# A gated state-space layer on one core: five fill banks and one bank for y, the fill three tiles ahead, 32-row pieces, and jobs in a new order

## The chip, the cores and the metric

One core of a Trainium2 chip runs the whole program. The time is the device time of that core in microseconds (us). A kernel's time is the median of several runs; the profile shows one further execution.

## The reference, cut to what matters

```python
xr, gate = jnp.split(x @ W_in.T, 2, axis=-1)            # x: (2, 2048, 512), 1024 channels each
xc = silu(causal_conv4(xr + t_emb, W_conv) + b_conv)    # depthwise, 4 taps
xn = (xc - mean) / sqrt(var + 1e-5) * ln_g + ln_b
Bm, Cm, dt = jnp.split(xn @ W_xproj.T, 3, axis=-1)      # 16 states each
Ad = 1.0 - tanh(A_log) * 0.01 * tanh(dt @ W_dt.T + b_dt)
Bd = Bm * minimum(norm(xn), 1.0)
# for each token t:
h = clip(h * ad[:, :, None] + bd[:, :, None] * xt[:, None, :], -10.0, 10.0)
y = einsum('bd,bdh->bh', ct, h) + D * xn
out = x + (y * silu(gate)) @ W_out.T
```

## The kernel before

The two sequences of 2048 tokens are cut into chunks of 128 tokens, taken in turn from the two sequences: 32 steps. `steps` runs the bodies for k = -2 to 32. In the body of step k the core does the scan of chunk k, and in the gaps the preparation of the chunks k+1 (the norm, the state at the chunk's head, the stacks) and k+2 (projection, convolution, statistics) and the output of chunk k-1. 30 steps (k = 0 to 29) hold all of this.

A step has 32 tiles, 8 blocks of 128 channels times 4 groups of 4 states. A tile goes through six stages, each counted by a semaphore:

- `fill` (L539, TensorE, PE): four matmuls from the row stack `xs` and the weights `ts` into one bank of `ps_fill`. They give the lower bound of the clipped scan.
- `copy_low` (L769, ScalarE, ACT) copies the bank to `low`.
- `widen` (L548, PE) adds the span to the same bank, which makes the upper bound.
- `scan` (L975, VectorE, DVE) runs the clipped scan over `low` and the bank.
- `weigh` (L1073, GpSimd, POOL) multiplies by C.
- `flip` (L575, PE) transposes four 128x128 blocks and adds them into `ps_y`. Before the tiles 0 and 16 it starts a half of y with `base` (L555), and before the tiles 12 and 16 it adds D times xn with `skip` (L561).

In iteration s PE runs widen(s+1), fill(s+2), the jobs of point 2s, flip(s-4) and the jobs of point 2s+1; ACT runs copy_low(s+2) and `side` of both points; DVE runs scan(s+1) and its `side`; POOL runs weigh(s) and one side instruction in some iterations. Every queue is in order. `ps_fill` has 4 banks and `fill` of a tile waits until the tile 4 before it was scanned. `ps_y` has 2 banks, one for each half (512 channels) of y. `gated` (L963, DVE) multiplies a half of y by the gate; `base` of a half waits until `gated` has read that half of the chunk before.

`JOBS` lists the other matmuls as (first point, parts, name, half, chunk offset, halves, bank of `ps_job`); a job's parts lie at successive points, and the share of its work in a part is worked out by integer division. A job waits until the job before it in its bank was taken. `TAKE` is the point at which ACT or DVE reads the result, `TAP_AT` the points at which ACT makes the eight channel blocks of the convolution's taps. The chunk k+1 side work on DVE is: z (L869, L873), zm (L900), the decay scan pf (L904), its reciprocal (L923), h0 (L919), bc (L927), the four nb instructions (L937 to L944), the clip of h1 (L931, point 28) and the carries (L955). `xt` is the transposed xc, from which z is made; ACT takes its second half at point 62 and the first gate job uses the same bank.

SyncE (SP) issues all transfers in one order. The stack `xs` of the next chunk is loaded in body k after `xh_done`: for each 32-token block two copies of `xh` rows 1 to 31 (L340, L341) and one of the 32 rows of `xl` (L345). Rows 0 and 32 of the stack hold ones, loaded once in `later_loads`. ACT's `carry` (L745) and DVE's (L955) write into the tiles `xh` and `xl`, so they wait for `xstack_in`. Further down SP issues the pieces of `ts` (L379, 31 and 32 rows), the carry rows (L383) and h16 (L388).

Of the kernel before, what the change touches and what calls it, by code (L numbers as in the profile page):

```python
# [26 lines left out]
P = 128  # L27
# [3 lines left out]
SUB = 32  # L31
NSUB = P // SUB
# [7 lines left out]
RING = 4  # L40
AHEAD = 2
LAG = 4
HOLD = 4
TAPRING = 4
# [27 lines left out]
xstack_in0 xstack_in1 stack_in0 stack_in1 bound_out bound_in0 bound_in1  # L72
# [13 lines left out]
def build(nc, A, out, scratch, r_dram, c_dram):  # L86
    F, H = mybir.dt.float32, mybir.dt.float16
    ALU, ACT = mybir.AluOpType, mybir.ActivationFunctionType
    with ExitStack() as S:
# [95 lines left out]
        ps_y = S.enter_context(nc.psum_tensor("ps_y", [P, 2, BANK], F))  # L185
        ps_job = S.enter_context(nc.psum_tensor("ps_job", [P, 2, BANK], F))

        def since(eng, name, value):

            if isinstance(value, int) and value <= 0:  # L190
# [7 lines left out]
        JOBS = [(1, 3, "z", 0, 1, 1, 1), (1, 4, "gate", 0, 0, 2, 0), (5, 1, "hend", 0, -1, 2, 1),  # L198
                (6, 4, "gate", 1, 0, 2, 0), (7, 1, "hend", 1, -1, 2, 1), (10, 1, "yT", 1, -1, 2, 1),
                (15, 1, "zT", 0, 1, 1, 1), (17, 4, "xr", 0, 2, 2, 0), (20, 1, "h0", 0, 1, 2, 1),  # L200
                (22, 4, "xr", 1, 2, 2, 0), (23, 1, "h0", 1, 1, 2, 1), (26, 1, "nb", 0, 1, 1, 1),
                (28, 12, "conv", 0, 2, 2, 0), (30, 1, "carry", 0, 1, 2, 1), (34, 1, "carry", 1, 1, 2, 1),
                (38, 14, "out", 0, -1, 1, 1), (44, 10, "conv", 1, 2, 2, 0), (54, 1, "yT", 0, 0, 2, 1),
                (57, 1, "xt", 0, 2, 2, 0), (60, 1, "xt", 1, 2, 2, 0)]
        LAST = {(name, i): first + parts - 1 for first, parts, name, i, *_ in JOBS}
        TAKE = {("z", 0): 4, ("gate", 0): 5, ("hend", 0): 5, ("hend", 1): 7, ("yT", 1): 10, ("gate", 1): 11,
                ("zT", 0): 15, ("h0", 0): 20, ("h0", 1): 23, ("xr", 0): 20, ("nb", 0): 26,
                ("xr", 1): 25, ("carry", 0): 30, ("carry", 1): 34, ("conv", 0): 42, ("out", 0): 52,
                ("conv", 1): 54, ("yT", 0): 54, ("xt", 0): 58, ("xt", 1): 62}
        TAP_AT = [22, 28, 32, 36, 38, 40, 44, 46]  # L210

        Z_AT = 12
        GATED_AT = (42, 8)
# [42 lines left out]
        N_FIXED = 16 * 9  # L256
# [17 lines left out]
        def _(sp):  # L274
# [14 lines left out]
            def later_loads():  # L289
# [4 lines left out]
                for p in range(2):  # L294
                    carry = A["carry"].rearrange("r (j c) -> r j c", j=NSUB)
                    loads.append((ts[96:128, p], carry))
                    for r in (0, 32):
                        loads.append((xs[r:r + 1, p], A["ones16"].rearrange("o (j d) -> o j d", j=NSUB)))
# [8 lines left out]
            def body(k, p):  # L307
# [21 lines left out]
                if exists(k, 1):  # L329
# [8 lines left out]
                    for jj in range(NSUB):  # L338
                        a = SUB * jj
                        sp.dma_start(xs[1:SUB, pn, jj], xh[a + 1:a + SUB]).then_inc(xstack, 16)  # L340
                        sp.dma_start(xs[SUB + 1:2 * SUB, pn, jj], xh[a + 1:a + SUB]).then_inc(xstack, 16)  # L341
# [4 lines left out]
                if exists(k, 1):  # L346
# [9 lines left out]
                    for h in range(2):  # L356
# [7 lines left out]
                                 ).then_inc(sem["c_in"], 16)  # L364
                    sp.wait_ge(sem["bound_out"], 48 * (j + 1))
# [35 lines left out]
        def _(pe):  # L401
# [123 lines left out]
            def fill(k, p, s):  # L525
# [3 lines left out]
                if s == 0:  # L529
                    if isinstance(k, int) and k == 0:  # L530
                        pe.wait_ge(sem["fixed_in"], N_FIXED)
                    pe.wait_ge(sem[f"xstack_in{p}"], N_XSTACK * pair(k, p, 0))
# [4 lines left out]
                o = ps_fill[:, s % RING].rearrange("d (n t) -> d n t", n=QN)  # L537
# [6 lines left out]
            def widen(k, p, s):  # L544
# [3 lines left out]
                mm(ps_fill[:, s % RING], pick[:], spans[:, p, q * BANK:(q + 1) * BANK], start=False, stop=True,  # L548
                   skip_group_check=True).then_inc(sem["bounded"], 1)

            def base(k, p, i):

                half = slice(i * BANK, (i + 1) * BANK)
                since(pe, "y_gated", 2 * (k - 1) + i + 1)
                mm(ps_y[:, i], mT[:, p], xn[:, p, half], start=True, stop=False)  # L555

            def skip(k, p, i):
# [3 lines left out]
                last = mm(ps_y[:, i], ident, xd[:, i * BANK:(i + 1) * BANK], start=False, stop=False)  # L561
# [3 lines left out]
            def flip(k, p, s):  # L565
# [8 lines left out]
                for e in range(QN):  # L574
                    last = mm(ps_y[:, u // 4, cut], prod[:, s % HOLD, e, :], ident, start=False,  # L575
# [30 lines left out]
        def _(act):  # L606
# [21 lines left out]
            def side(k, p, point):  # L628
# [47 lines left out]
                if point == 12 and exists(k, 2):  # L676
# [24 lines left out]
                if point == 24 and exists(k, 1):  # L701
# [418 lines left out]
```

## Time and profile before

| | us |
|---|---|
| median of 3 runs (2226.87 to 2229.91) | 2229.75 |
| the profiled execution | 2229.9 |
| its span, first to last instruction | 2228.1 |

| engine | busy us | share of the span |
|---|---|---|
| PE matmul | 2016.9 | 91% |
| POOL | 1818.6 | 82% |
| DVE | 1762.9 | 79% |
| ACT | 1434.6 | 64% |

Busy times of PE count pipelined matmuls until their modelled ends, so the start-to-start distances in a timeline tell its work better than the busy column. "Idle before, releaser" names what an engine's instruction waited for. The granted clock was 1.0 of full (2.4 GHz) but for the first part of the run.

### The profile page before, as it was taken

The numbers are of one execution on the slowest core, as the hardware profiler recorded it, in microseconds if no ns is written. First come the engines' busy times: TensorE is split into PE (matmuls) and PEld (weight loads), VectorE is DVE, ScalarE is ACT, GpSimd is POOL, SyncE is SP. The second block draws the span as 40 slices with busy tenths as digits, with TensorE's granted clock in tenths as the row PEclk, the third lists the DMA queues.
The fourth block names the chain that finished last, engine by engine and source line by source line (L and its number), as shares of the span: only waits on it lengthen the run. The fifth ranks groups of instructions, "written<-read, shape, count | busy, mean of one in ns | idle before, by whom it ended". The sixth has DMA issues, their size and how long they took to land.

```text
span 2228.1 us, 47105 instructions
## 1 busy us (share of the span) xinstructions
PE 2016.9 (91%) x16976; PEld 1458.5 (65%) x16976; DVE 1762.9 (79%) x2080; ACT 1434.6 (64%) x3462; POOL 1818.6 (82%) x1444
## 2 busy tenths in 40 slices
PE   5599999999999999999999999999999999999888
PEld 4366666666666666666666666666666666666654
DVE  2388888788888788888788888788888878888886
ACT  4576666676666676666666666666666667666642
POOL 1288888888888888888888898888888888888876
PEclk8599999999999999999999999999999999999999
DMA  4111111121111121111111111111111112111110
GB/s 164 51 56 42 53 40 51 57 61 46 49 41 51 56 60 46 50 41 51 56 60 47 51 45 46 55 60 56 44 53 40 53 59 61 40 55 39 46 53 15
DMA packets 77777, 117.05 MB, mean 53 GB/s; under 512 B 17941, under 2 KB 46997, under 8 KB 72933
## 3 DMA queue, kind: packets, MB, share of 16 engines
q1 hardware_dynamic: 77544, 114.04, 16.5%
q8 instruction: 135, 2.21, 0.4%
q14 instruction: 98, 0.79, 0.1%
HBM read 59.47 MB, written 9.18 MB: 31 GB/s over the span
## 4 chain that ended last, share of the span: by engine, by line
PE 35%; SPq 23%; ACT 13%; DMA 12%; issue 8%; DVE 6%; POOL 2%; DVEq 0%; POOLq 0%; ACTq 0%
DMA xs<-xl 11%; SPq L340 9%; SPq L341 9%; PE ps_job L490 7%; PE ps_y L575 6%; SPq L345 5%; PE ps_job L449 5%; PE ps_fill L548 4%; ACT low L769 4%; ACT tap L728 4%; PE ps_fill L539 3%; DVE ks L975 3%; PE ps_job L456 2%; PE ps_job L462 2%; POOL prod L1073 2%
## 5 line engine op out<-in xcount | busy, mean ns | idle before, releaser
L1073 POOL TENSOR_TENSOR prod<-ks,crep 128x512 f32<-128x512 f32 x1024 | 1305.1, 1288 | 292.3 <-PE ps_y L575 265.6
L975 DVE TENSOR_TENSOR_SCAN ks<-low,ps_fill 128x512 f32<-128x512 f32 x1024 | 1227.7, 1210 | 284.1 <-PE ps_fill L548 274.6
L769 ACT COPY low<-ps_fill 128x512 f32<-128x512 f32 x1024 | 594.0, 580 | 594.4 <-PE ps_fill L539 588.3
L575 PE MATMUL ps_y<-c_sb,prod 128*128 128x128 f32 x4096 | 621.3, 274 | 0.7 <-POOL prod L1073 0.6
L575 PEld LDWEIGHTS ps_y<-c_sb,prod 128*128 128x128 f32 x4096 | 465.9, 141 | 113.1 <-issue 50.9
L548 PE MATMUL ps_fill<-spans,pick 128*128 128x512 f16 x1024 | 393.2, 384 | 121.1 <-ACT low L769 117.1
L539 PEld LDWEIGHTS ps_fill<-ts,xs 128*128 128x128 f16 x4096 | 314.4, 98 | 150.2 <-issue 4.9
L539 PE MATMUL ps_fill<-ts,xs 128*128 128x128 f16 x4096 | 397.0, 219 | 2.9 <-DMA xs<-h 2.9
L548 PEld LDWEIGHTS ps_fill<-spans,pick 128*128 128x128 f16 x1024 | 99.3, 97 | 236.4 <-ACT low L769 193.7
L728 ACT ACTIVATE tap<-xr,cols_sb 128x128 f32<-128x128 f32 x768 | 251.7, 392 | 0.1
L444 PE MATMUL ps_job<-x,w_in 128*128 128x128 f16 x3072 | 215.2, 221 | 15.3 <-POOL x L1043 7.8
L490 PE MATMUL ps_job<-w_out,yT 128*128 128x512 f16 x768 | 208.7, 383 | 1.5 <-DVE yT L891 1.5
L449 PE MATMUL ps_job<-w_in,x 128*128 128x512 f16 x768 | 209.4, 382 | 0.1
L444 PEld LDWEIGHTS ps_job<-x,w_in 128*128 128x128 f16 x3072 | 188.4, 99 | 24.3 <-issue 23.3
L462 PE MATMUL ps_job<-c_sb,tap 128*128 128x128 f32 x1024 | 160.0, 281 | 15.5 <-ACT tap L728 9.7
L462 PEld LDWEIGHTS ps_job<-c_sb,tap 128*128 128x128 f32 x1024 | 121.6, 145 | 42.9 <-ACT tap L728 18.7
L728 ACT ACTIVATE tap<-xr,conv_b,cols_sb 128x128 f32<-128x128 f32 x256 | 123.0, 481 | 0.0
L490 PEld LDWEIGHTS ps_job<-w_out,yT 128*128 128x128 f16 x768 | 70.5, 99 | 36.9 <-issue 3.0
L449 PEld LDWEIGHTS ps_job<-w_in,x 128*128 128x128 f16 x768 | 72.9, 107 | 31.9 <-issue 1.1
L1046 POOL TENSOR_TENSOR h<-h 16x1024 f16<-16x1024 f32 x32 | 68.1, 2128 | 19.2 <-ACT h L713 19.2
L931 DVE TENSOR_SCALAR h<-h 16x1024 f32<-16x1024 f32 x32 | 82.3, 2573 | 0.0
L955 DVE SCALAR_TENSOR_TENSOR xl<-xh,c_sb,ps_job 128x512 f16<-128x512 f16 x64 | 47.8, 747 | 43.3 <-ACT lend L747 43.3
(126 smaller groups left out, 2373.1 us busy)
## 6 DMA issues: line engine op xcount, KB each, us to landing
crep<-c_dram SPq DMA_DIRECT2D x32, 1024.0 KB, 4.7
xs<-xh SPq DMA_DIRECT2D x256, 62.0 KB
xs<-xl SPq DMA_DIRECT2D x224, 64.0 KB
xf<-in_xT SPq DMA_DIRECT2D x32, 256.0 KB, 2.8
res<-in_x SPq DMA_DIRECT2D x32, 256.0 KB, 2.7
out_dram<-res SPq DMA_DIRECT2D x32, 256.0 KB, 2.1
ts<-tth SPq DMA_DIRECT2D x128, 32.0 KB
ts<-tth SPq DMA_DIRECT2D x128, 31.0 KB
```

Of the source, the lines that this page charges most:

```text
L340: sp.dma_start(xs[1:SUB, pn, jj], xh[a + 1:a + SUB]).then_inc(xstack, 16)
L444: last = mm(ps[:, e * P:(e + 1) * P], w_in[:, a, c, d:d + P], x16[:, q, b, c, :], start=(c == n == 0), stop=(c == CB - 1 and n == 2))
L449: last = mm(ps, x16[:, q, a, c, :], w_in[:, b, c, DI + i * BANK:DI + (i + 1) * BANK], start=(c == n == 0), stop=(c == CB - 1 and n == 2))
L462: last = mm(ps[:, e * P:(e + 1) * P], tap[:, d % TAPRING, v], ident, start=(v == 0), stop=(v == TAPS - 1), is_transpose=True)
L490: last = mm(ps, yT[:, a, c, :], w_out[:, b, c, :], start=(c == n == 0), stop=(c == DB - 1 and n == 2))
L539: last = mm(o[:, :, SUB * jj:SUB * (jj + 1)], xs[:, p, jj, u * P:(u + 1) * P], ts[:, p, jj, q * QN * SUB:(q + 1) * QN * SUB].rearrange("s ...
L548: mm(ps_fill[:, s % RING], pick[:], spans[:, p, q * BANK:(q + 1) * BANK], start=False, stop=True, skip_group_check=True).then_inc(sem["bou ...
L575: last = mm(ps_y[:, u // 4, cut], prod[:, s % HOLD, e, :], ident, start=False, stop=(u % 4 == 3 and q == 3 and e == QN - 1), is_transpose= ...
L728: last = act_fn(tap[:, d % TAPRING, v], xr[:, p, d, v:v + P], ACT.Identity, scale=cols[:, d, 3 + v:4 + v], bias=conv_b[:, p, d:d + 1] if v ...
L769: copy(low[:, s % RING], ps_fill[:, s % RING]).then_inc(sem["low_copied"], 1)
L975: nc.vector.tensor_tensor_scan(ks[:, u % 2, QN * q:QN * (q + 1)].rearrange("d n t -> d (n t)"), low[:, s % RING], ps_fill[:, s % RING], 0. ...
L1073: tt(prod[:, i % HOLD], ks[:, u % 2, part], crep[:, p, part], ALU.mult).then_inc(sem["weighed"], 1)
```

## The change

- `RING` 4 to 5 banks for `ps_fill`, `ps_y` from two banks to one that both halves use in turn; `base` of a half now waits until `gated` has read the half before it. Bank and `low` buffer go by the running tile number.
- `AHEAD` 2 to 3: in iteration s PE runs fill(s+3) and ACT copy_low(s+3).
- The `xh` pieces of the stack become 32 rows from row 0; two transfers of a row of ones then overwrite rows 0 and 32 in every step (semaphore `ones_in`), issued behind crep; four loads fewer at the start. PE's first fill of a chunk waits for `ones_in`.
- `TAPRING` 4 to 3 buffers.
- `JOBS`, `TAKE`, `TAP_AT` and `GATED_AT` get new points; so do five side instructions.

```diff
 EPS = 1e-5
-RING = 4
-AHEAD = 2
+RING = 5
+AHEAD = 3
...
 HOLD = 4
-TAPRING = 4
+TAPRING = 3
...
 res_in out_done0 out_done1 const_in fixed_in
-xstack_in0 xstack_in1 stack_in0 stack_in1 bound_out bound_in0 bound_in1
+xstack_in0 xstack_in1 ones_in0 ones_in1 stack_in0 stack_in1 bound_out bound_in0 bound_in1
...
         ps_fill = S.enter_context(nc.psum_tensor("ps_fill", [P, RING, BANK], F))
-        ps_y = S.enter_context(nc.psum_tensor("ps_y", [P, 2, BANK], F))
+        ps_y = S.enter_context(nc.psum_tensor("ps_y", [P, BANK], F))
...
-        JOBS = [(1, 3, "z", 0, 1, 1, 1), (1, 4, "gate", 0, 0, 2, 0), (5, 1, "hend", 0, -1, 2, 1),
-                (6, 4, "gate", 1, 0, 2, 0), (7, 1, "hend", 1, -1, 2, 1), (10, 1, "yT", 1, -1, 2, 1),
-                (15, 1, "zT", 0, 1, 1, 1), (17, 4, "xr", 0, 2, 2, 0), (20, 1, "h0", 0, 1, 2, 1),
-                (22, 4, "xr", 1, 2, 2, 0), (23, 1, "h0", 1, 1, 2, 1), (26, 1, "nb", 0, 1, 1, 1),
-                (28, 12, "conv", 0, 2, 2, 0), (30, 1, "carry", 0, 1, 2, 1), (34, 1, "carry", 1, 1, 2, 1),
-                (38, 14, "out", 0, -1, 1, 1), (44, 10, "conv", 1, 2, 2, 0), (54, 1, "yT", 0, 0, 2, 1),
+        JOBS = [(3, 2, "z", 0, 1, 1, 1), (1, 4, "gate", 0, 0, 2, 0), (6, 1, "hend", 0, -1, 2, 1),
+                (6, 4, "gate", 1, 0, 2, 0), (8, 1, "hend", 1, -1, 2, 1), (10, 1, "yT", 1, -1, 2, 1),
+                (15, 1, "zT", 0, 1, 1, 1), (19, 4, "xr", 0, 2, 2, 0), (21, 1, "h0", 0, 1, 2, 1),
+                (24, 4, "xr", 1, 2, 2, 0), (24, 1, "h0", 1, 1, 2, 1), (26, 1, "nb", 0, 1, 1, 1),
+                (33, 11, "conv", 0, 2, 2, 0), (30, 1, "carry", 0, 1, 2, 1), (35, 1, "carry", 1, 1, 2, 1),
+                (40, 13, "out", 0, -1, 1, 1), (46, 9, "conv", 1, 2, 2, 0), (54, 1, "yT", 0, 0, 2, 1),
...
         LAST = {(name, i): first + parts - 1 for first, parts, name, i, *_ in JOBS}
-        TAKE = {("z", 0): 4, ("gate", 0): 5, ("hend", 0): 5, ("hend", 1): 7, ("yT", 1): 10, ("gate", 1): 11,
-                ("zT", 0): 15, ("h0", 0): 20, ("h0", 1): 23, ("xr", 0): 20, ("nb", 0): 26,
-                ("xr", 1): 25, ("carry", 0): 30, ("carry", 1): 34, ("conv", 0): 42, ("out", 0): 52,
-                ("conv", 1): 54, ("yT", 0): 54, ("xt", 0): 58, ("xt", 1): 62}
-        TAP_AT = [22, 28, 32, 36, 38, 40, 44, 46]
+        TAKE = {("z", 0): 5, ("gate", 0): 5, ("hend", 0): 6, ("hend", 1): 8, ("yT", 1): 10, ("gate", 1): 11,
+                ("zT", 0): 15, ("h0", 0): 21, ("h0", 1): 24, ("xr", 0): 23, ("nb", 0): 26,
+                ("xr", 1): 28, ("carry", 0): 30, ("carry", 1): 35, ("conv", 0): 44, ("out", 0): 53,
+                ("conv", 1): 55, ("yT", 0): 54, ("xt", 0): 58, ("xt", 1): 62}
+        TAP_AT = [24, 26, 32, 36, 39, 42, 45, 49]
...
         Z_AT = 12
-        GATED_AT = (42, 8)
+        GATED_AT = (39, 7)
...
         N_CONST = 16 * 5
-        N_FIXED = 16 * 9
+        N_FIXED = 16 * 5
+        N_ONES = 16 * 2
...
                     loads.append((ts[96:128, p], carry))
-                    for r in (0, 32):
-                        loads.append((xs[r:r + 1, p], A["ones16"].rearrange("o (j d) -> o j d", j=NSUB)))
...
                         a = SUB * jj
-                        sp.dma_start(xs[1:SUB, pn, jj], xh[a + 1:a + SUB]).then_inc(xstack, 16)
-                        sp.dma_start(xs[SUB + 1:2 * SUB, pn, jj], xh[a + 1:a + SUB]).then_inc(xstack, 16)
+                        sp.dma_start(xs[0:SUB, pn, jj], xh[a:a + SUB]).then_inc(xstack, 16)
+                        sp.dma_start(xs[SUB:2 * SUB, pn, jj], xh[a:a + SUB]).then_inc(xstack, 16)
...
                                  ).then_inc(sem["c_in"], 16)
+                    sp.wait_ge(xstack, N_XSTACK * pair(k, p, 1))
+                    for r in (0, SUB):
+                        sp.dma_start(xs[r:r + 1, pn], A["ones16"].rearrange("o (j d) -> o j d", j=NSUB)
+                                     ).then_inc(sem[f"ones_in{pn}"], 16)
...
                         pe.wait_ge(sem["fixed_in"], N_FIXED)
-                    pe.wait_ge(sem[f"xstack_in{p}"], N_XSTACK * pair(k, p, 0))
+                    pe.wait_ge(sem[f"ones_in{p}"], N_ONES * pair(k, p, 0))
...
                 since(pe, "scanned", g - RING + 1)
-                o = ps_fill[:, s % RING].rearrange("d (n t) -> d n t", n=QN)
+                o = ps_fill[:, g % RING].rearrange("d (n t) -> d n t", n=QN)
...
                 pe.wait_ge(sem["low_copied"], TILES * k + s + 1)
-                mm(ps_fill[:, s % RING], pick[:], spans[:, p, q * BANK:(q + 1) * BANK], start=False, stop=True,
+                mm(ps_fill[:, (TILES * k + s) % RING], pick[:], spans[:, p, q * BANK:(q + 1) * BANK], start=False, stop=True,
...
                 half = slice(i * BANK, (i + 1) * BANK)
-                since(pe, "y_gated", 2 * (k - 1) + i + 1)
-                mm(ps_y[:, i], mT[:, p], xn[:, p, half], start=True, stop=False)
+                since(pe, "y_gated", 2 * k + i)
+                mm(ps_y[:], mT[:, p], xn[:, p, half], start=True, stop=False)
...
                     pe.wait_ge(sem["xd_done"], k + 1)
-                last = mm(ps_y[:, i], ident, xd[:, i * BANK:(i + 1) * BANK], start=False, stop=False)
+                last = mm(ps_y[:], ident, xd[:, i * BANK:(i + 1) * BANK], start=False, stop=False)
...
                 for e in range(QN):
-                    last = mm(ps_y[:, u // 4, cut], prod[:, s % HOLD, e, :], ident, start=False,
+                    last = mm(ps_y[:, cut], prod[:, s % HOLD, e, :], ident, start=False,
...
                     copy(zm[0:1, 0], z[0:1, 0:2 * NS]).then_inc(sem["zm_high"], 1)
-                if point == 12 and exists(k, 2):
+                if point == 13 and exists(k, 2):
...
                     copy(p_end[:, 1 - p:2 - p], pf[:, 1, P - 1:P]).then_inc(sem["p_kept"], 1)
-                if point == 24 and exists(k, 1):
+                if point == 21 and exists(k, 1):
...
                     act.wait_ge(sem["filled"], TILES * k + s + 1)
-                    copy(low[:, s % RING], ps_fill[:, s % RING]).then_inc(sem["low_copied"], 1)
+                    copy(low[:, (TILES * k + s) % RING], ps_fill[:, (TILES * k + s) % RING]).then_inc(sem["low_copied"], 1)
...
                 j, q = k + 1, (p + 1) % 2
-                if point == 46 and exists(k, 2):
+                if point == 48 and exists(k, 2):
...
                     nc.vector.bn_stats(st[:, 0], xc[:, 0:BANK]).then_inc(sem["stats"], 1)
-                if point == 56 and exists(k, 2):
+                if point == 57 and exists(k, 2):
...
                         ).then_inc(sem["z_taken"], 1)
-                if point == 6 and exists(k, 1):
+                if point == 7 and exists(k, 1):
...
                 dve.wait_ge(sem["gate_taken"], 2 * k + i + 1)
-                tt(gate[:, half], ps_y[:, i], gate[:, half], ALU.mult).then_inc(sem["y_gated"], 1)
+                tt(gate[:, half], ps_y[:], gate[:, half], ALU.mult).then_inc(sem["y_gated"], 1)
...
                     nc.vector.tensor_tensor_scan(ks[:, u % 2, QN * q:QN * (q + 1)].rearrange("d n t -> d (n t)"),
-                                                 low[:, s % RING], ps_fill[:, s % RING], 0.0,
+                                                 low[:, g % RING], ps_fill[:, g % RING], 0.0,
...
                         tt(xn[:, p], xn[:, p], row_b[:], ALU.add).then_inc(sem["xn_done"], 1)
-                    if s == 9 and exists(k, 0):
+                    if s == 11 and exists(k, 0):
...
                             pool.wait_ge(sem["xa"], k + 2)
```

## Rows read from the trace of the kernel before

**Rows 1.** The waits over the run: who waited for whom, us, times, longest us.
```profile
POOL prod L1073 <- PE ps_y L575: 265.6, 281, 2.2
...
PE ps_fill L548 <- ACT low L769: 117.1, 183, 2.0
ACT xh L745 <- DMA xs<-xl: 68.7, 32, 10.1
```

**Rows 2.** Busy time by engine over one step (columns PE, PEld, DVE, ACT, POOL, PEclk).
```profile
1032.60:1099.03 66.43, 61.80 (x530) 44.84 (x531) 54.43 (x65) 44.33 (x109) 56.69 (x46) 1.00 0.17 51
```

**Rows 3.** Timeline of PE in step 13: start, us, group, idle before and its releaser.
```profile
979.41 0.38 PE L548 MATMUL ps_fill<-spans,pick 128*128 128x512 f16 x1
...
995.05 0.83 PE L444 MATMUL ps_job<-x,w_in 128*128 128x128 f16 x12
...
1004.36 0.39 PE L548 MATMUL ps_fill<-spans,pick 128*128 128x512 f16 x1 [0.73 <-ACT low L769]
...
1010.50 1.08 PE L555 MATMUL ps_y<-xn,mT 128*128 128x512 f32 x2
...
1012.27 0.60 PE L575 MATMUL ps_y<-c_sb,prod 128*128 128x128 f32 x4
1012.71 0.81 PE L490 MATMUL ps_job<-w_out,yT 128*128 128x512 f16 x3
1013.36 0.38 PE L548 MATMUL ps_fill<-spans,pick 128*128 128x512 f16 x1
1013.57 0.39 PE L539 MATMUL ps_fill<-ts,xs 128*128 128x128 f16 x4
1013.80 0.61 PE L575 MATMUL ps_y<-c_sb,prod 128*128 128x128 f32 x4
...
1032.52 0.39 PE L548 MATMUL ps_fill<-spans,pick 128*128 128x512 f16 x1 [1.05 <-ACT low L769]
```

**Rows 4.** Timeline of DVE in the same step.
```profile
981.16 0.69 DVE L891 SCALAR_TENSOR_TENSOR yT<-ps_job,yT 128x512 f16<-128x512 f32 x1
...
982.89 0.88 DVE L900 TENSOR_TENSOR zm<-z,zm 1x32 f16<-1x32 f32 x1
...
985.94 0.40 DVE L904 TENSOR_TENSOR_SCAN pf<-ad,spans 16x127 f32<-16x127 f32 x1
...
987.38 0.92 DVE L923 RECIPROCAL pf<-pf 16x128 f32<-16x128 f32 x1
...
990.03 0.73 DVE L919 SCALAR_TENSOR_TENSOR h<-h,first_decay,ps_job 16x512 f32<-16x512 f32 x1 [0.42 <-PE ps_job L471]
...
991.97 1.37 DVE L927 TENSOR_TENSOR bc<-zT,pf 16x256 f32<-16x256 f32 x1
...
997.27 0.15 DVE L937 TENSOR_SCALAR nbh<-ps_job 128x16 f16<-128x16 f32 x1
...
998.38 1.21 DVE L975 TENSOR_TENSOR_SCAN ks<-low,ps_fill 128x512 f32<-128x512 f32 x1
999.50 2.64 DVE L931 TENSOR_SCALAR h<-h 16x1024 f32<-16x1024 f32 x1
...
1003.96 0.75 DVE L955 SCALAR_TENSOR_TENSOR xl<-xh,c_sb,ps_job 128x512 f16<-128x512 f16 x1 [0.69 <-ACT lend L747]
...
1014.91 0.67 DVE L963 TENSOR_TENSOR gate<-ps_y,gate 128x512 f32<-128x512 f32 x1
```

**Rows 5.** One line over the run: minimum, median, maximum duration in ns.
```profile
L873 DVE SCALAR_TENSOR_TENSOR z<-z,tiny,sums x32: 402/1223/1287, 53.4 to 2105.9; 128x48 f32<-128x48 f32 x32
```

**Rows 6.** Timeline of SP in the same step: its transfer instructions.
```profile
988.70 2.44 SPq L341 DMA_DIRECT2D xs<-xh  x1
991.19 4.36 SPq L345 DMA_DIRECT2D xs<-xl  x4
```

**Rows 7.** Timeline of ACT: at the end of the same step.
```profile
1030.75 1.24 ACT L644 ACTIVATE xn<-xc,tiny 128x1024 f32<-128x1024 f32 x1 [0.57 <-DVE tiny L864]
```

**Rows 8.** Timeline of ACT: before the first step.
```profile
80.33 0.58 ACT L745 CAST xh<-ps_job 128x512 f16<-128x512 f32 x1 [10.10 <-DMA xs<-xl]
```
## The prediction, made before the result was known

> **What bounds the kernel now.** I read the waits first, then the busy times of one step, then the timelines of PE and DVE through one step. The waits [rows 1] show POOL standing 266 us for `flip` on PE, and PE standing 117 us before `widen` for ACT's copy. So PE is the engine the others wait for, and ACT's lateness is what stops it. The busy times [rows 2] say how far the rest is: POOL 56.7 and DVE 54.4 of a step of 66.4 us. No engine is full.
>
> PE's own work comes from start-to-start distances [rows 3]: widen 0.21, fill 0.23, flip 0.44, so 0.88 a tile; a part of out or gate 0.65; base and skip 1.77 together (1010.50 to 1012.27), and 0.88 each. An xr group's 0.83 overlaps the next by 0.16, as out's 0.81 does: 0.67. Other groups of four transposes I take at flip's 0.44. A step: 32 x 0.88 + 16 x 0.65 + 8 x 0.67 + 14 x 0.44 (conv, xt, yT, hend) + 1.8 (z's 16 matmuls at 0.11) + 3.5 (base, skip) + 2.6 (h0, carry) + 0.8 (nb, zT) = 58.8 (28.2, 10.4, 5.4, 6.1 come first). PE therefore stands some 7.6 us a step.
>
> I cut the step into three legs at places that the change moves [rows 3]: start of iteration 0 to iteration 5 (979.41; its start is 1032.52 - 66.45 = 966.07): 13.3. Iteration 5 to base(1) (1010.50): 31.1. base(1) to the end (1032.52): 22.0.
>
> **The change, part by part.**
>
> *Fill three ahead, five banks.* widen(s+1) is now issued two iterations after its fill, so a late copy of up to one iteration costs PE nothing. Of the 7.6 us this covers all waits for ACT's copy, 117.1 / 32 = 3.7 by the wait list, 1.05 and 0.73 of it in the two rows shown [rows 1, 3]; cover gone, it is those 3.7. The fifth bank only pays for the distance: fill(s+3) needs scan(s-2), as fill(s+2) did. What is late next is the question, below.
>
> *32-row pieces.* A 31-row piece of 62 KB held SP 2.44 us, while four 32-row pieces of 64 KB took 4.36 together, the first of them still behind the backlog [rows 6]. Eight pieces at 0.6 instead of four at 0.6 and four at 2.4 free SP some 7 us a step, and the stack lands before ACT asks for it: its carry waited 68.7 us in 32 waits [rows 1], DVE 0.69 behind it [rows 4]. In the steady step these waits are part of the ones above. Before the first step nothing hides them: ACT stood 10.1 us [rows 8]. SP is also the road from there to the first fill, so I take 11 off the start (bounds 6, if another queue is next, and 14). The ones: two small transfers more a step on SP's queue, past which the ts pieces, carry rows and h16 move by about 1 us. SP stands there for POOL's ttl anyway, so nothing.
> The Trainium skill (DMA: Bandwidth & Descriptors, Why a DMA increments its semaphore by 16 and not by 1) says that a copy is spread over the largest number of engines up to 16 that divides its outer dimension, and 31 rows leave one. If the slow issue were instead due to bytes, the new pieces would keep 2.4 and the 11 us would be 0; on the 64 KB pieces the trace agrees with the skill's rule.
>
> *One bank for y.* Before, base(1) ran at 1010.50, over 4 us before gated(0) at 1014.91 [rows 3, 4]. With one bank it must come after it. So everything in DVE's queue up to point 39 now lies on the road to base(1), flip(16) and all behind. This is the part that gives back.
>
> *Jobs, taps.* With the integer division, PE's iterations cost (start of iteration 0 = 0): 1.53, 3.03, 2.38, 2.62, 3.48, hence iteration 5 at 13.04. Iterations 5 to 19: 1.32, 0.88, 1.2, 0.88, 1.55, 2.97, 1.55, 2.97, 2.72, 0.88, 1.53, 1.74, 1.97, 0.88, 1.32; with widen and fill, PE could be at base(1) at 37.8. Behind it: 3.69 - 0.44 for iteration 20, then 1.97, 1.53, 1.53, 2.62, 1.97, 1.97, 1.76, 1.32, 0.88, 1.32, 0.88, together 21.0. Three taps' buffers are enough: each block's conv part lies before the point of the tap that reuses it. yT(0) finds out taken, hend finds z taken, xr (point 19) finds x16 low: waits that before made up the rest of the 7.6.
>
> **Leg by leg.**
>
> *Iteration 5 to base(1).* DVE's scan(6) starts 0.42 behind widen. Then DVE has, up to gated(0): 15 scans at 1.12 (998.38 to 999.50) = 16.8, and side work, durations less the 0.07 by which they overlap: yT 0.62, zm 0.81, pf 0.33, reciprocal 0.85, h0 2 x 0.66, bc 1.30, nb 1.11, clip 2.57, carry 2 x 0.68, gated 0.67: 10.9 [rows 4]. With 0.2 for ACT's yT copy and 0.13 back to PE: 28.5. PE's own road is 24.8, so DVE decides and PE stands 3.7 (some of it earlier, where fill waits for scan). POOL is ahead of flip throughout: xd moves from iteration 9 to 11, away from xl. The leg was 31.1.
>
> *base(1) to the end.* PE alone, 21.0; was 22.0, though conv parts and an out part worth 1.5 have moved into it.
>
> *Start to iteration 5.* PE's 13.04, plus a new wait. The first gate job needs the bank that ACT empties with xt's second half. ACT's xn [rows 7] needs the statistics; DVE can't start them before scan(29) is done (2.85 before iteration 0), then about 1.1 for them (an estimate: no longer than gated's 0.67 and three instructions of 0.15), scan(30) and 0.2: xn starts at -0.42. Then 1.15 for it, 0.47 for a copy, 0.6 for xt: 1.9, where PE asks at 0.88. So 1.0. Before, widen's 1.05 stood there instead [rows 3]: that wait only changes its name. Bounds 0 and 2.0. gated(1) at point 7 ends 1 us before base(0) asks.
>
> Sum: 14.1 + 28.5 + 21.0 = 63.6, against 66.4: 2.8 a step. Thirty full steps give 84, the step after them about as much as one (3), the last nothing, the start 11: 98. The profiled execution took 2229.9 (1.8 more than its span), so 2132; it stands 0.15 above the median of the runs, which changes nothing. I put the forecast at 2136, since every handover left out can only add.
>
> **The bound of the unknown.** DVE's instructions with two SBUF inputs have no fixed price: L873 took 402 ns where POOL was idle and 1223 in the middle, up to 1287 [rows 5]. Where in POOL's work each falls changes with the order. I take that spread, 0.8, for the four of this leg: zm, bc and the clip (0.81, 1.30, 2.57) look as if they pay it now and may lose it, pf (0.33) can only gain it, and the clip may pay it twice. So the leg of 28.5 lies between 26.1 and 30.1, worth 74 us and 50 us of the run; up to 0.7 more if DVE still waits for ACT's carry.
> The Trainium skill (SBUF — State Buffer, Who interferes with whom) calls this an exclusive lock on a port pair that DVE and GpSimd share, held for a whole instruction; by it a POOL with fewer gaps makes DVE's share dearer. With pf and half of the clip's second payment that is 1.2 more, 64.8 a step, which saves 1.6 x 31 + 11 = 61 and gives 2169; without the rule the sum stays 2132. L873's two durations (402 and 1223 ns) agree with the rule.
>
> **Rivals.**
> - *PE decides* (the y bank never makes it wait, because DVE's two-input instructions shorten, or DVE runs less late than summed): step 58.8 + 1.0 = 59.8, gain 6.6 x 31 + 11 = 216: 2014; halfway 2075. For it: POOL and DVE are both under 57 busy. Against: DVE's stretch has hardly a gap in the rows. Chance of under 2095: 10%.
> - *Half is lost*: DVE's instructions at their upper price, or ACT's taps, carry and reciprocal wait (its bounds job moves from point 24 to 21, where it stands for DVE's reciprocal) reach PE: step 65 to 65.6: 2170 to 2195. Chance 15%.
> - *Slower*: the handover of the one y bank. DVE stands in its own queue for PE's h0(1) and nb, which now share bank 1 two points apart, so that DVE comes to point 39 later than summed. The price is 1 us a step for each us; it decides from 98 / 31 = 3.2 us, base(1) at 31.7 or more behind iteration 5. For it: the two do wait on each other there. Against: the sum has PE's nb 1 us before DVE wants it. About 2240. Chance 4%, and 2% for within 0.2%.
> - *The change does nothing in the steady step*, the waits only changing name: 2230 - 11 = 2219. Chance 3%.
>
> **How the numbers follow.** The likeliest case, 66%, has its own range 2105 to 2168. With the part of the second rival up to 2188 and of the first down to 2092 it makes the range. 0.2% (4.5 us) is what a measurement of this kernel can tell. Faster 0.94, within 0.02, slower 0.04.
>
> **What the profile after should show.** Step length 63.6. PE's waits for `copy_low` near nothing. A wait of PE before L555 on DVE L963, at base(1) alone, 2 to 4 us a step, with DVE free of gaps from iteration 5 on. A wait of 1 us before the first L449 on ACT L739. All xs pieces issued in 0.6. ACT's L745 no longer behind a DMA. First fill 11 us earlier. Wrong would be: a wait before L555 twice a step, flip waiting for POOL, or DVE with gaps while PE stands.

## The result

| | us |
|---|---|
| before, median of 4 runs (2226.87 to 2229.91) | 2228.45 |
| after, median of 4 runs (2255.19 to 2266.64) | 2263.66 |
| ratio, with its 95% interval | 1.0152 (1.013 to 1.0174) |
| span of the profiled execution after | 2263.7 |

The change made the kernel slower by 1.5%. I had forecast 2136, 4% faster, and at the most 2188.

### The profile page after: what moved, and what is told of

It is laid out like the page before. It is cut to its first block, busy times and chain, and to the rows that moved or that the text cites. A ratio compares the mean times of both kernels' runs of the same rounds, so it can differ in the third digit from the quotient of the medians.

```text
span 2263.7 us, 47166 instructions
## 1 busy us (share of the span) xinstructions
PE 2018.2 (89%) x16976; PEld 1486.0 (66%) x16976; DVE 1771.9 (78%) x2080; ACT 1428.9 (63%) x3462; POOL 1805.1 (80%) x1444
## 4 chain that ended last, share of the span: by engine, by line
PE 69%; DVE 15%; issue 11%; ACT 4%; POOL 1%; SPq 1%; DMA 0%; DVEq 0%; POOLq 0%; ACTq 0%
PE ps_y L578 13%; DVE ks L978 9%; PE ps_job L447 8%; PE ps_job L452 8%; PE ps_job L493 7%; PE ps_fill L551 7%; PE ps_fill L542 7%; PE ps_y L558 4%; PE ps_job L465 4%; DVE h L934 3%; PE ps_job L459 2%; PE ps_job L474 2%; PE ps_y L564 2%; PE ps_job L487 1%; PE ps_job L483 1%
## 5 line engine op out<-in xcount | busy, mean ns | idle before, releaser
L1076 POOL TENSOR_TENSOR prod<-ks,crep 128x512 f32<-128x512 f32 x1024 | 1291.9, 1279 | 357.1 <-PE ps_y L578 268.1
L558 PE MATMUL ps_y<-xn,mT 128*128 128x512 f32 x128 | 93.8, 824 | 68.3 <-DVE gate L966 68.3
L934 DVE TENSOR_SCALAR h<-h 16x1024 f32<-16x1024 f32 x32 | 134.3, 4196 | 0.0
L452 PEld LDWEIGHTS ps_job<-w_in,x 128*128 128x128 f16 x768 | 71.5, 104 | 62.5 <-issue 31.0
L479 PE MATMUL ps_job<-xh,bqm 128*128 128x512 f16 x128 | 48.9, 382 | 66.2 <-DVE xl L958 65.4
L748 ACT CAST xh<-ps_job 128x512 f16<-128x512 f32 x64 | 38.1, 595 | 94.2 <-PE ps_job L479 94.2
```

What stands on the lines that cost most here:

```text
L452: last = mm(ps, x16[:, q, a, c, :], w_in[:, b, c, DI + i * BANK:DI + (i + 1) * BANK], start=(c == n == 0), stop=(c == CB - 1 and n == 2))
L934: tsc(h1[:], h1[:], CLIP, -CLIP, ALU.min, ALU.max).then_inc(sem["h1_done"], 1)
L1076: tt(prod[:, i % HOLD], ks[:, u % 2, part], crep[:, p, part], ALU.mult).then_inc(sem["weighed"], 1)
```

## The profile after

From the page: the engines, the granted clock in 40 slices, and four groups (busy us, mean ns, idle before).

```profile
PE 2018.2 (89%) x16976; PEld 1486.0 (66%) x16976; DVE 1771.9 (78%) x2080; ACT 1428.9 (63%) x3462; POOL 1805.1 (80%) x1444
...
PEclk8799999999999999999999999999999999999999
...
L1076 POOL TENSOR_TENSOR prod<-ks,crep 128x512 f32<-128x512 f32 x1024 | 1291.9, 1279 | 357.1 <-PE ps_y L578 268.1
L978 DVE TENSOR_TENSOR_SCAN ks<-low,ps_fill 128x512 f32<-128x512 f32 x1024 | 1221.3, 1206 | 385.9 <-PE ps_fill L551 383.0
...
L558 PE MATMUL ps_y<-xn,mT 128*128 128x512 f32 x128 | 93.8, 824 | 68.3 <-DVE gate L966 68.3
...
L934 DVE TENSOR_SCALAR h<-h 16x1024 f32<-16x1024 f32 x32 | 134.3, 4196 | 0.0
```

PE's busy time in total is that of before. Two groups have grown: `base` (L558), from 606 to 824 ns for each of its 128 instructions, and the clip of h1 (L934, the old L931), from 2573 to 4196 ns in the mean. The mean granted clock fell from 0.984 to 0.968. The tenths of the PEclk line don't show it: the stretches below do.

The waits over the run (us in total, times, longest):

```profile
POOL prod L1076 <- PE ps_y L578: 268.1, 200, 4.2
...
PE ps_y L558 <- DVE gate L966: 68.3, 32, 2.3
PE ps_job L479 <- DVE xl L958: 65.4, 31, 2.1
...
PE ps_job L452 <- ACT xcT L742: 22.7, 31, 0.8
```

ACT's copies no longer stop PE. Three new waits stand in their place: before `base` for `gated`, before `carry` for DVE's L958 (the old L955), and before the first gate job for ACT's xt.

One step in the three legs of the prediction (us, then busy by engine, PEclk, DMA share):

```profile
1042.07:1055.98 13.91, 13.17 (x98) 8.96 (x96) 9.81 (x12) 7.14 (x13) 12.37 (x9) 1.00 0.01 1
1055.98:1086.95 30.97, 25.89 (x269) 20.21 (x267) 29.59 (x34) 23.37 (x65) 28.63 (x25) 1.00 0.22 63
1086.95:1110.33 23.38, 23.01 (x168) 16.58 (x169) 15.39 (x20) 13.66 (x32) 15.30 (x14) 0.93 0.24 63
sum 68.26, PE 62.06 PEld 45.76 DVE 54.79 ACT 44.18 POOL 56.30; mean PE 20.69 PEld 15.25 DVE 18.26 ACT 14.73 POOL 18.77
```

The legs are 13.9, 31.0 and 23.4 us: 68.3, where they were 13.3, 31.1 and 22.0. In the third the granted clock is 0.93 of full. The clock record has one stretch at half speed (1.2 GHz), 3.4 us long, in each of the full steps but the first, here from 1086.84. By itself, and what follows it (the granted clock is the column behind POOL's):

```profile
1086.80:1090.20 3.40, 3.25 (x4) 1.40 (x5) 1.12 (x1) 1.35 (x2) 0.25 (x1) 0.50 0.12 30
1090.20:1110.33 20.13, 19.76 (x165) 15.21 (x164) 14.41 (x19) 12.46 (x30) 15.21 (x13) 1.00 0.25 68
```

PE around base(1) in that step:

```profile
1078.53 0.60 PE L465 MATMUL ps_job<-c_sb,tap 128*128 128x128 f32 x4
1081.24 0.38 PE L479 MATMUL ps_job<-xh,bqm 128*128 128x512 f16 x1 [2.11 <-DVE xl L958]
...
1086.95 2.04 PE L558 MATMUL ps_y<-xn,mT 128*128 128x512 f32 x2 [2.26 <-DVE gate L966]
1088.78 1.73 PE L564 MATMUL ps_y<-xc,c_sb 128*128 128x512 f32 x2
1090.35 0.60 PE L578 MATMUL ps_y<-c_sb,prod 128*128 128x128 f32 x4
```

PE stands 2.11 us before carry(1) and 2.26 before base(1), both for DVE. Then base and skip take 3.40 us (1086.95 to 1090.35), where they took 1.77 [rows 3]. They run at the half clock.

DVE in the same step:

```profile
1052.62 0.27 DVE L876 SCALAR_TENSOR_TENSOR z<-z,tiny,sums 128x48 f32<-128x48 f32 x1
...
1059.41 0.89 DVE L903 TENSOR_TENSOR zm<-z,zm 1x32 f16<-1x32 f32 x1
...
1067.62 1.17 DVE L930 TENSOR_TENSOR bc<-zT,pf 16x256 f32<-16x256 f32 x1
...
1071.06 1.22 DVE L978 TENSOR_TENSOR_SCAN ks<-low,ps_fill 128x512 f32<-128x512 f32 x1 [0.50 <-PE ps_fill L551]
...
1073.87 1.22 DVE L978 TENSOR_TENSOR_SCAN ks<-low,ps_fill 128x512 f32<-128x512 f32 x1 [0.26 <-PE ps_fill L551]
1075.00 4.32 DVE L934 TENSOR_SCALAR h<-h 16x1024 f32<-16x1024 f32 x1
1079.26 1.20 DVE L978 TENSOR_TENSOR_SCAN ks<-low,ps_fill 128x512 f32<-128x512 f32 x1
...
1086.15 0.65 DVE L966 TENSOR_TENSOR gate<-ps_y,gate 128x512 f32<-128x512 f32 x1
```

Against [rows 4], zm is the same, bc 0.2 shorter, z1 (L876) 0.27 instead of some 1.2. So of the instructions that the prediction bounded by L873's spread only the clip has become dearer: it takes 4.32 us instead of 2.64, and it stands in DVE's queue in front of scan(16) to scan(20), both carries and gated.

The start went as forecast and better: the second tile's widen of step 0 begins 14.3 us earlier. The pieces are issued in 0.6 each (SP, same step):

```profile
1059.08 0.59 SPq L340 DMA_DIRECT2D xs<-xh  x1
```

## The experiments

All are compared with the kernel before on the same chip. Theory A in the expectations is that the clip, which stands in DVE's queue ahead of the one y bank's handover, is the main cause; the other theories are told there. "Step" is the distance from one step's second scan to the next one's, in the middle of the run.

| kernel | step us | median us | ratio to before (95%) | half-clock stretch, of 29 steps |
|---|---|---|---|---|
| before | 66.5 | 2228 to 2231 | 1 | 0 |
| after | 68.3 | 2263.66 | 1.0152 (1.013 to 1.0174) | 29 |
| clip_late | 63.5 | 2125.78 | 0.9533 (0.9519 to 0.9548) | 0 |
| gap_filled | 65.1 or 65.8 | 2178.77 | 0.9769 (0.9753 to 0.9786) | 8 |
| two_y_ahead2 | 67.3 | 2242.17 | 1.0053 (1.0038 to 1.0068) | 0 |
| rows32_only | 65.5 | 2183.97 | 0.9794 (0.978 to 0.9809) | 0 |
| clip_late_gap_filled | 62.5 | 2096.61 | 0.9397 (0.9383 to 0.9411) | 0 |
| two_y_ahead2_clip_late | 66.6 | 2222.15 | 0.9961 (0.9948 to 0.9974) | 0 |
| rows32_clip_late | 65.8 | 2193.45 | 0.9836 (0.982 to 0.9853) | 0 |
| banks_old_order | 66.6 or 67.3 | 2234.77 | 1.0022 (1.0013 to 1.0032) | 19 |
| pool_lets_clip | 64.4 or 66.1 | 2164.9 | 0.9712 (0.9698 to 0.9727) | 7 |
| tth_later | 65.6 or 67.3 | 2210.91 | 0.9916 (0.9901 to 0.9931) | 12 |
| gate_later_too | 62.0 | 2079.55 | 0.9327 (0.9312 to 0.9343) | 0 |
| pieces_of_31 | 68.3 | 2277.13 | 1.021 (1.0189 to 1.0231) | 26 |

"a or b" are the medians of the steps without and with such a stretch. The 29 steps are the full ones but the first.

### Is it the clip in front of the one y bank? (clip_late)

```diff
-                if point == 28 and exists(k, 1):      # DVE, clip of h1
+                if point == 40 and exists(k, 1):
-                if point == 41 and exists(k, 1):      # ACT, h16 high
+                if point == 43 and exists(k, 1):
-                    if s == 21 and exists(k, 1):      # POOL, h16 low
+                    if s == 22 and exists(k, 1):
```

> The changed kernel with the clip of h1 on DVE moved from point 28 to point 40, behind gated(0), and h16's two halves two points later. Theory A (the clip, which takes 4.3 us while POOL is busy, stands in DVE's queue in front of the one y bank; its lateness makes PE stand before base(1), and the stand makes the clock fall): iteration 5 to base(1) falls from 31.0 us to about 26, no wait at base(1), granted clock 1.0 all through the steps, step 61 to 62.5 instead of 68.3, total 2050 to 2095. Theory B (the handover of the one y bank costs this whatever the clip does): step stays above 66, total above 2190.

Measured: 2125.78, step 63.5, no half-clock stretch. The total is 31 us above theory A's range and far below theory B's. The stand before carry(1) is gone. The stand before base(1) stays, but shorter:

```profile
PE ps_y L558 <- DVE gate L966: 42.2, 32, 1.6
```

The clip itself, behind gated where POOL is waiting for PE, takes 0.65 us (minimum, median, maximum in ns):

```profile
L934 DVE TENSOR_SCALAR h<-h x32: 654/654/676, 74.1 to 2041.2; 16x1024 f32<-16x1024 f32 x32
```

The clip moved, with its two readers behind it, turns 1.5% slower into 4.7% faster. So the clip's place is the main cause, as theory A says, but its numbers were missed: the step was set 1 to 2.5 us too low, and the stand at the handover is 1.3 us, not 0.

### Does the stand make the clock fall? (gap_filled)

```diff
-                (33, 11, "conv", 0, 2, 2, 0), ... (40, 13, "out", 0, -1, 1, 1),
+                (33, 8, "conv", 0, 2, 2, 0), ... (39, 14, "out", 0, -1, 1, 1),
```

> The changed kernel with the first half's conv parts (33, 8 parts) and out (39, 14 parts) begun earlier, so that PE has about 1.1 us of work inside its stand before base(1). Theory A (a stand of 2.3 us makes the clock fall for 3.4 us, which costs 1.7 a step): the stand is cut in pieces of about 1 us, the clock stays at 1.0, step 65 to 66, total 2160 to 2195. Theory B (the clock falls for another reason, or would fall anyway): only the 1.1 us of moved work, step 67.2, total about 2230.

Measured: 2178.77. 21 of 29 steps have no half-clock stretch and take 65.1; 8 have one and take 65.8. PE hardly stands before base(1) any more (1.6 us in the whole run, where it was 68.3), but the stand before carry(1) is still there:

```profile
PE ps_job L479 <- DVE xl L958: 67.0, 32, 2.1
```

Theory A holds for most steps, and the 8 show that the one stand left is sometimes enough. Of the 3.2 us a step between 68.3 and 65.1 I put 1.7 down to the clock, its price in pool_lets_clip below; that leaves 1.5 for the work moved. This split is worked out, not measured.

### What are banks, look-ahead and order worth? (two_y_ahead2, rows32_only, banks_old_order)

```diff
 two_y_ahead2, against after
-RING = 5
-AHEAD = 3
+RING = 4
+AHEAD = 2
-        ps_y = S.enter_context(nc.psum_tensor("ps_y", [P, BANK], F))
+        ps_y = S.enter_context(nc.psum_tensor("ps_y", [P, 2, BANK], F))
...
```

> The changed kernel with four fill banks, two y banks and the fill two tiles ahead, as before; the new order and the 32-row pieces stay. Theory A (the one y bank behind a late DVE is what loses): no stand at base(1), clock 1.0, waits for ACT's copy back at 3 to 4 us a step, step 65 to 66.5, total 2165 to 2210. Theory C (the new order of jobs is itself the loss): total at or above 2250.

Measured: 2242.17, step 67.3, slower than before too, so theory A's range was missed by 32 us and C's by 8: neither holds as it was written. PE doesn't stand at the y bank. But the clip is 3.98 us here as well, PE stands 1.4 us before carry(1), and ACT's copies stop PE again:

```profile
PE ps_fill L551 <- ACT low L772: 144.6, 270, 2.3
```

rows32_only is the kernel before with the parts of the diff on `xs`, `ones_in` and `N_FIXED`, and no other.

> The kernel before with the 32-row pieces and the ones alone. If the pieces do what the sum says: first fill 11 to 14 us earlier, ACT's carry no longer waits for a transfer, and of PE's 0.73 us wait behind it at most that comes back in each step: step 65.7 to 66.4, total 2192 to 2216. If other waits take its place in the step, only the start is gained: 2214.

Measured: 2183.97, 2.1% faster. The start is 11 us earlier, as expected. But the step is 1.0 shorter (65.45), where I had allowed 0.73 at most, and the last, lighter step 2.4, so the total lies 8 us under the range. ACT's carry (L748) no longer waits for a transfer, and PE's waits for copies fall from 117 [rows 1] to 94 us, 0.7 of the 1.0 a step:

```profile
PE ps_fill L551 <- ACT low L772: 94.3, 153, 2.0
...
ACT xh L748 <- PE ps_job L479: 7.7, 32, 0.6
```

The page of before had shown how much hung on these pieces. In the chain of work that ended last (its part 4), the issuing queue and the transfers hold 35% between them:

```profile
PE 35%; SPq 23%; ACT 13%; DMA 12%; issue 8%; DVE 6%; POOL 2%; DVEq 0%; POOLq 0%; ACTq 0%
```

banks_old_order is after with the jobs, takes, taps and side points of before; `gated` stays at 39 and 7.

> The changed kernel with the jobs, taps and side points of before; only gated stays at 39 and 7. With the order of before the clip meets the POOL work that it met there (2.66 us instead of 4.3), and conv and out parts lie ahead of base(1). Theory A: the one bank's stand is short, the clock does not fall, and look-ahead pays: step 63 to 65, total 2110 to 2165. If the new points are what makes one bank bearable, the step is 66.5 or more: total at or above 2200.

Measured: 2234.77, step 66.6 or 67.3, which misses theory A's range by 70 us and lies where the other theory had it. Against 65.5 for rows32_only, banks and look-ahead lose 1.1 us a step, and more where the clock falls. The clip rose here too, to 3.9 us (median), against my assumption that the order sets it: the new order alone (two_y_ahead2) and the new banks alone each lengthen it. PE stands before carry(1):

```profile
PE ps_job L479 <- DVE xl L958: 77.3, 32, 2.5
```

### The same with the clip out of the way (two_y_ahead2_clip_late, rows32_clip_late, clip_late_gap_filled)

Each carries the edit of clip_late; in the old order the clip goes to point 43 and h16 to 45 and iteration 23.

> two_y_ahead2 (new order, 32-row pieces, four fill banks, two y banks, two tiles ahead) with the clip behind gated(0). Theory: the fill three ahead is worth PE's waits for ACT's copy (4.5 us a step in two_y_ahead2) less the handover of the one y bank (1.3). Then this lies between: step 64.5 to 66, total 2150 to 2200, slower than clip_late (2126). If banks and look-ahead are worth nothing once the clip is out of the way, it is at 2126 too.

Measured: 2222.15, step 66.6. PE waits for ACT's copies 5.1 us a step:

```profile
PE ps_fill L551 <- ACT low L772: 163.6, 298, 2.3
```

Against clip_late (63.5), five banks, one y bank and the fill three ahead are worth 3.1 us a step, once the clip is out of the way; in the old order, with the clip in place, they cost 1.1.

> rows32_only (2184) with the clip moved behind gated(0) (point 43), h16 at point 45. In the old order the clip took 2.66 us and PE waits for the ACT copies behind DVE's nb and carry. If the clip's late end is what delays the carries and scans there, the step falls from 65.45 to 64 to 65: total 2140 to 2170. If ACT's own queue makes the copies late, nothing changes: 2180 to 2190.

Measured: 2193.45, step 65.8: 0.3 longer, so neither range was hit. In the old kernel moving the clip gains nothing: the queue behind it was not on PE's road.

> The changed kernel with both edits: clip behind gated(0), conv and out begun earlier. clip_late has a step of 63.5 us and still stands 1.3 us a step before base(1). If that stand is the plain handover (flip's end, gated 0.66, back to PE), the moved work fills most of it: step 62.4 to 62.9, total 2092 to 2112. If DVE's queue is still what comes late, the moved work only changes places: step 63.3 or more, total at or above 2118.

Measured: 2096.61, step 62.5. The work moved into the handover is worth the 1.0 us expected, which speaks for the 1.3 us being the plain handover.

### Why does the clip take 4.3 us? (pool_lets_clip, tth_later)

POOL in the changed kernel while the clip stands (DVE, 1075.00 to 1079.32):

```profile
1074.66 0.66 POOL L1052 TENSOR_TENSOR bnd<-ad,bnd 16x254 f16<-16x254 f32 x1
1075.28 1.26 POOL L1076 TENSOR_TENSOR prod<-ks,crep 128x512 f32<-128x512 f32 x1
1076.51 1.03 POOL L1059 TENSOR_TENSOR tth<-nbh,c_sb 128x512 f16<-128x512 f16 x1
1077.51 1.27 POOL L1076 TENSOR_TENSOR prod<-ks,crep 128x512 f32<-128x512 f32 x1
1080.53 1.26 POOL L1076 TENSOR_TENSOR prod<-ks,crep 128x512 f32<-128x512 f32 x1 [1.75 <-DVE ks L978]
```

and in the kernel before (clip 999.50 to 1002.14 [rows 4]):

```profile
999.34 1.26 POOL L1073 TENSOR_TENSOR prod<-ks,crep 128x512 f32<-128x512 f32 x1
1000.57 1.03 POOL L1056 TENSOR_TENSOR tth<-nbh,c_sb 128x512 f16<-128x512 f16 x1
1001.57 3.05 POOL L1073 TENSOR_TENSOR prod<-ks,crep 128x512 f32<-128x512 f32 x2
```

In both, the clip ends 0.55 us after a POOL instruction: before after tth (1001.60), after after weigh(15) (1078.78). In the other runs where it meets POOL it is 0.54 to 0.55 too, so its own work (0.65 where it is undisturbed) seems to begin about as that instruction ends. What differs is how early weigh(15) could have run. It needs flip(11) from PE, here before and after:

```profile
1000.80 0.60 PE L575 MATMUL ps_y<-c_sb,prod 128*128 128x128 f32 x4
1075.42 0.60 PE L578 MATMUL ps_y<-c_sb,prod 128*128 128x128 f32 x4
```

Before, flip(11) ended at 1001.40, 0.2 us ahead of tth; the clip went first, and weigh(15), the first of the two in the last row, took 1.72 us instead of 1.27. After, PE is ahead: flip(11) ended at 1076.02, 1.5 us ahead of tth, and weigh(15) went first (0.5 to 1.5 ahead in every other run where the clip lost to it). The clip then got in because weigh(16) needs scan(16), which stands behind the clip. That the early flip decides is the reading that fits all of these steps; no run moves the flip alone.

```diff
 pool_lets_clip
                         h = s // 4 - 3
+                        if s == 14:
+                            pool.wait_ge(sem["h1_done"], j + 1)
```

> The changed kernel with one wait more: in iteration 14 POOL waits for the clip of h1 before it makes tth. The clip stays at point 28. Theory A (the clip needs a port that POOL holds from instruction to instruction, so it starts only where POOL pauses; the look-ahead took away the pause): the clip starts behind weigh(14) and takes 1.5 to 2.3 us instead of 4.3, iteration 5 to base(1) is 2 us shorter, the stand before base(1) too short for the clock to fall, step 63.8 to 65, total 2125 to 2165. Theory B (the clip is long for a reason of its own place in DVE's queue): clip stays at 4.3, POOL only loses time: total 2264 or more.

Measured: the clip takes 2.1 us and the step is 64.4 without a half-clock stretch:

```profile
L934 DVE TENSOR_SCALAR h<-h x32: 672/2095/2118, 67.6 to 2068.8; 16x1024 f32<-16x1024 f32 x32
```

Two steps in a row, without and with such a stretch (PEclk is the column behind POOL's):

```profile
934.45:998.86 64.41, 60.34 (x529) 45.18 (x529) 52.54 (x66) 44.16 (x110) 56.28 (x46) 1.00 0.18 53
998.86:1064.87 66.01, 61.94 (x529) 45.77 (x529) 52.55 (x66) 44.13 (x110) 56.29 (x46) 0.97 0.19 52
```

2164.9 in all. An added wait makes the kernel 4.4% faster than the changed one. Theory A holds for the clip: with 2.2 us less of it, iteration 5 to base(1) is 2.2 shorter. For the stand it was wrong. What has gone is the stand of 2.11 before carry(1); the one before base(1) is as long as before:

```profile
PE ps_y L558 <- DVE gate L966: 69.8, 32, 2.3
```

So base(1) stands 2.3 us with a clip of 2.1 or of 4.3 in front, and 1.3 with none; the rest of the long clip is paid before carry(1). With the second stand alone the clock still falls, in 7 of 29 steps. Such a stretch costs 1.6 to 1.7 us in a step.

```diff
 tth_later
-                    if s in (14, 18) and exists(k, 1):
-                        h = s // 4 - 3
+                    if s in (17, 18) and exists(k, 1):
+                        h = s - 17
```

> The changed kernel with POOL's tth moved from iteration 14 to 17, so that only weigh(14) and weigh(15) stand between the clip's arrival and POOL's pause. Theory A: the clip takes 1.0 us less (3.3), the step 1.0 less (67.3), and 1.7 less again if the stand before base(1) gets too short for the clock to fall (65.6): total 2175 to 2235. Theory B: clip unchanged, total 2260 or more.

Measured: 2210.91, step 65.6 without a stretch, 67.3 with, both as theory A had them. The clip is shorter by tth's 1.0 us:

```profile
L934 DVE TENSOR_SCALAR h<-h x32: 917/3324/3346, 68.3 to 2114.7; 16x1024 f32<-16x1024 f32 x32
```

### What was left (gate_later_too, pieces_of_31)

```diff
 gate_later_too, against clip_late_gap_filled
-                (1, 4, "gate", 0, ...), (6, 4, "gate", 1, ...)   takes 5 and 11
+                (2, 4, "gate", 0, ...), (8, 4, "gate", 1, ...)   takes 6 and 12
```

> clip_late_gap_filled (step 62.5) with the gate jobs moved to points 2 to 5 and 8 to 11 and their takes to 6 and 12, so that the first of them no longer asks for its bank while ACT still writes xn and takes xt. If the stand of 0.9 us there is on the road: step 61.6 to 62.0, total 2065 to 2085. If POOL (56.3 us of work) or DVE's queue before zm now decides, no change or worse: 2090 to 2110.

Measured: 2079.55, step 62.0: some half of the 0.9 us stand came back. This is the fastest version, 6.7% under before. POOL still waits for PE:

```profile
POOL prod L1076 <- PE ps_y L578: 151.3, 221, 4.2
```

> The changed kernel with the 31-row pieces of before. If the pieces are worth here what they are worth in the old order (start 11 us, 1.0 a step): total 2300 to 2315. If in the new order the stack still lands in front of the carries, only the start: about 2275.

Measured: 2277.13, as expected for the start alone. In the changed kernel the 32-row pieces are worth the start (14 us) and nothing in the step; 26 of 29 steps have a half-clock stretch (68.3), three have none (66.6).

## Why the prediction was wrong

| leg | predicted | measured |
|---|---|---|
| start to iteration 5 | 14.1 | 13.9 |
| iteration 5 to base(1) | 28.5 | 31.0 |
| base(1) to the end | 21.0 | 23.4 |
| earlier start of the run | 11 | 14.3 |

**The bound and the mechanism** were right: PE's waits for ACT's copies went, the new one before the first gate job (0.9 for 1.0) came, and DVE decides when base(1) can start. The sum missed the step by 4.7 us (68.3 for 63.6): 1.7 for the clip, 0.8 for other waits of DVE, 1.6 for the clock and 0.6 for a bank make it up.

**The term that was mis-sized** is the clip in the second leg, put at 2.57 and measured at 4.3. The prediction had even named the shared port, but gave it 0.8 us at a time, "and the clip may pay it twice", from L873's spread. That step failed in two ways. The spread was read wrong: L873's 402 ns are not those of an idle POOL, for POOL's add from 51.42 ended at 53.77 and L873, begun at 53.43, at 53.83, right behind it. And L873, zm and bc read two tiles and in the full steps of the changed kernel wait only for the POOL instruction that is running, while the clip reads one tile and lost to POOL three times running. In the step above bc (1067.62) took 1.17 in the middle of four weighs without a gap:

```profile
1064.79 5.14 POOL L1076 TENSOR_TENSOR prod<-ks,crep 128x512 f32<-128x512 f32 x4
```

So no price could be carried over from L873 to the clip. The clip's follows from POOL's queue: it ended behind the last POOL instruction that was ready well ahead. Before, PE's late flip broke the row after tth; the change, in its order and in its banks alike, took that break away. The rest of that leg's miss, about 0.8, are DVE's waits for PE at scan(14), scan(15) and nb, 0.50 and 0.26 of it in the rows above. pool_lets_clip shows the size: with the clip at 2.1 the step is 64.4 for 63.6 summed.

**The term that was missing** is the clock. The sum had PE stand 3.7 us and then go on at full speed. The stand of 2.26 us behind one of 2.11, 4.4 together for the summed 3.7, is followed by 3.4 us at 1.2 GHz, in which base and skip take 3.40 instead of 1.77: 1.6 of the 2.4 us by which the third leg was short. Another 0.6 is iteration 30, where xt's second half waits for its bank.
The rows of before could not show the fall: in its full steps PE had no stand above 1.1 us (the 2.0 in [rows 1] lies outside them). What they could show is that the sum puts one long stand where there were many short ones.

**The rivals.** The slower one named the right place, base(1) behind a late DVE, but the wrong cause: in the rows above DVE has no wait before h0(1) and 0.1 before nb, where 3.2 were asked for. "Half is lost" had the port, with a cap on its price. The chance of 4% for slower came from that cap.

**The 32-row pieces**: in the old kernel the start gains the 11 us that I had put down, in the changed one 14. In the old kernel they are also worth 1.0 a step, which I had counted among the copies' waits.

**The new order**: with two y banks and two tiles ahead it is slower than the old one (67.3 against 65.5), and still with the clip late (66.6 against 65.8). With the new banks and the clip in place the two orders are level (66.6 each in steps without a half-clock stretch). Whether the new order is worth anything with the new banks and the clip late isn't shown: the old order was never run so.

## What to carry to other kernels

When two stages that used to hand over through two buffers get one, write down what stands in the second engine's queue before the handover: all of it is now on the road. A DVE instruction that lengthens beside POOL has no price of its own, and one kind's can't be taken from another's: read for each how many POOL instructions in a row it sat through. The clip here got in only where POOL's next instruction was not ready, so a change that keeps POOL supplied lengthens it; put such an instruction where POOL must wait for somebody. And price a stand of PE twice: its length, and what may run behind it at half clock.

## What the runs showed of the hardware that I had not expected

- The same 16x1024 clip on DVE took 0.65 us with POOL waiting, and 2.1, 2.6, 3.3 and 4.3 us where one, two, two and three POOL instructions ran, whole or nearly so, before it ended. In the changed kernel DVE's instructions with two input tiles (zm, bc, L876) got in behind the one that was running, but for one bc at the end of the run (2.6 us). The Trainium skill (SBUF — State Buffer, Who interferes with whom) has the exclusive lock, held for one instruction and won by whoever issues first. The clip's record doesn't fit that: it starts at 1075.00, weigh(14)'s at 1075.28, and weigh(14), tth and weigh(15) all ended before it.
- One stretch at half clock, 3.4 us long, in each of 29 steps with two stands of PE, 2.11 and 2.26 us, and 3.5 us of work between them (26 of 29 with nearly the same stands in pieces_of_31). With stands of 1.1 and 2.3 (tth_later) in 12 of 29; with the second alone (pool_lets_clip) in 7, with the first alone (gap_filled) in 8, with one of 2.45 (banks_old_order) in 19; in none where the longest was 1.4 (two_y_ahead2) or 1.3 (clip_late).
- A stretch costs 1.7 us where it meets base and skip, and 0.75 where it meets other work (gap_filled, banks_old_order).
